# Other SBUF places for the operands of the matmuls of a non-local block

## The reference: what is computed

```
q = theta_w . x + theta_b                    (256 x 1024 positions)
xpool = maxpool2(x)                          (1024 x 256 positions)
k = phi_w . xpool + phi_b                    (256 x 256)
v = g_w . xpool + g_b                        (256 x 256)
p = softmax(q^T k / sqrt(256))               (1024 x 256)
out = z_w . (v p^T) + z_b + x                (1024 x 1024 positions)
```

## The kernel before, in words

| matmuls | stationary | moving | columns |
|---|---|---|---|
| project_q | theta 2 | x_split 3.5 | 512 |
| attend | vt 3.5 | pt 5 | 512 |
| project_out | z 2 | att 5 | 256 |
| project_k | phi 2 | xp 3.5 | 256 |
| project_v | xp 3.5 | g 2 | 256 |
| scores | q 3.5 | k 3.5 | 256 |

## Time and profile before

### The profile page before, as it was taken

The page is one execution under the profiler, slowest core; times in us unless marked ns, Lnnn a source line. Parts: engine busy times, 40 slices in busy tenths (PEclk is TensorE's granted clock), DMA queues, the critical chain, the costliest instruction groups (busy, mean ns, idle before and its releaser), DMA issues.

```text
span 2107.2 us, 41473 instructions
## 1 busy us (share of the span) xinstructions
PE 2084.7 (99%) x14030; PEld 1900.6 (90%) x14030; DVE 1562.8 (74%) x2620; ACT 1294.2 (61%) x2228; POOL 1372.8 (65%) x833
## 2 busy tenths in 40 slices
PE   8899999999999999999999999999999999999997
PEld 7799999999999999999999999999999999999997
DVE  8786776876777867767767778777678677787765
ACT  5566565665666665666656656656666556566553
POOL 4676666776667766666766667666667666676653
PEclk9999999999999999999999999999999999999999
DMA  6556556555566565566564665555665656655535
GB/s 220 176 179 208 170 205 219 189 189 200 169 210 236 166 204 172 196 219 200 180 210 164 210 229 171 203 179 184 219 211 177 209 168 200 229 174 204 184 117 180
DMA packets 212904, 407.22 MB, mean 193 GB/s; under 512 B 12688, under 2 KB 15760, under 8 KB 212880
## 3 DMA queue, kind: packets, MB, share of 16 engines
q1 hardware_dynamic: 212736, 406.90, 57.5%
q10 hardware_dynamic: 144, 0.01, 0.0%
HBM read 272.64 MB, written 134.22 MB: 193 GB/s over the span
## 4 chain that ended last, share of the span: by engine, by line
PE 94%; DVE 3%; POOL 1%; issue 1%; DMA 1%; ACT 1%; DVEq 0%; SPq 0%; ACTq 0%
PE bank L800 94%; DVE pt_raw L633 1%; DMA x<-x 1%; DVE x_top L651 0%; DVE x_bot L651 0%; POOL x_split_lo L520 0%; POOL att_f L533 0%; DVE g_lo L597 0%; POOL att_lo L538 0%; DVE x_split_lo L682 0%; ACT probs L432 0%; PE bank L807 0%; DVE att_f L664 0%; DVE q_lo L611 0%; POOL pt_lo L530 0%
## 5 line engine op out<-in xcount | busy, mean ns | idle before, releaser
L520 POOL TENSOR_TENSOR x_split_lo<-x,x_split_hi 128x1024 fp32r<-128x1024 f32 x254 | 612.6, 2418 | 265.0 <-ACT x_split_hi L335 260.2
L800 PE MATMUL bank<-att_hi,z_hi 128*128 128x256 f32 x1792 | 496.3, 277 | 7.8 <-DVE x_bot L651 4.9
L800 PE MATMUL bank<-att_lo,z_hi 128*128 128x256 f32 x1792 | 495.3, 276 | 0.0
L800 PE MATMUL bank<-att_hi,z_lo 128*128 128x256 f32 x1792 | 495.2, 276 | 0.0
L633 DVE STREAM_TRANSPOSE pt_raw<-probs 32x256 f32<-32x256 f32 x1024 | 446.2, 436 | 18.0 <-ACT probs L432 1.5
L800 PE MATMUL bank<-x_split_hi,theta_hi 128*128 128x512 f32 x1024 | 406.8, 397 | 3.2 <-POOL x_split_lo L520 1.7
L800 PE MATMUL bank<-x_split_lo,theta_hi 128*128 128x512 f32 x1024 | 404.1, 395 | 0.0
L800 PE MATMUL bank<-x_split_hi,theta_lo 128*128 128x512 f32 x1024 | 403.3, 394 | 0.0
L651 DVE TENSOR_TENSOR x_top<-bank,x_top 128x512 f32<-128x512 f32 x512 | 334.5, 687 | 83.1 <-PE bank L800 76.3
L538 POOL TENSOR_TENSOR att_lo<-att_f,att_hi 128x512 fp32r<-128x512 f32 (+1 forms) x192 | 282.9, 1480 | 173.8 <-ACT att_hi L374 173.8
L335 ACT ACTIVATE x_split_hi<-x 128x1024 fp32r<-128x1024 f32 x256 | 270.8, 1058 | 151.6 <-PE bank L800 146.1
(11 more groups left out here) (70 smaller groups left out, 4108.5 us busy)
## 6 DMA issues: line engine op xcount, KB each, us to landing
x<-x SPq DMA_DIRECT2D x256, 512.0 KB, 3.9
x_top<-x SPq DMA_DIRECT2D x128, 512.0 KB, 7.1
x_bot<-x SPq DMA_DIRECT2D x128, 512.0 KB, 5.5
out<-x_top SPq DMA_DIRECT2D x128, 512.0 KB, 3.6
out<-x_bot SPq DMA_DIRECT2D x128, 512.0 KB, 6.7
x_top<-theta_wt SPq DMA_DIRECT2D x4, 256.0 KB, 6.6
x_top<-g_wt SPq DMA_DIRECT2D x4, 256.0 KB, 6.3
x_bot<-z_wt SPq DMA_DIRECT2D x4, 256.0 KB, 6.8
```

The lines of the kernel that those rows point to most:

```text
L520: nc.gpsimd.tensor_tensor(flat(lo), flat(x_chunk(s, c)), raw(flat(hi)), ALU.subtract).then_inc(x_ready, 1)
L800: last = nc.tensor.matmul(dst, stationary(a), moving(b), start=start and n == 0, stop=stop and n == len(PRODUCTS) - 1, skip_group_check=re ...
```

## The change

The order in which the tensors are placed is another one, with a pad of 64 bytes at the start and one of 128 bytes behind g. `still` gets 224 columns in place of 256, and the matmuls of `keep_busy` as many. Nothing else differs: no instruction is added, removed or moved. By the same rules of placing, the places after are:

| matmuls | stationary | moving | columns |
|---|---|---|---|
| project_q | theta 0 | x_split 0 | 512 |
| attend | vt 0 | pt 0 | 512 |
| project_out | z 0 | att 3 | 256 |
| project_k | phi 0 | xp 3 | 256 |
| project_v | xp 3 | g 6 | 256 |
| scores | q 0 | k 3 | 256 |

The tensors that only the other engines use (x, x_top, x_bot, pooled, probs, pt_raw, att_f) come to 0 as well; they were at 3.5, and pt_raw and att_f at 5. The biases, maxima and sums come to between 3 and 6.

```diff
--- before.py
+++ after.py
@@ -65,6 +65,7 @@
 P1, P2, P6, P5, P7, P3, P4 = range(7)
 A_TOP, U_TOP, C11, V_BOT, C22, C12, C21 = range(7)
 SUMS = 14
+STILL = 224
 
 
 def non_local_block(nc, x, theta_wt, phi_wt, g_wt, z_wt, biases, out):
@@ -89,35 +90,37 @@
             return ctx.enter_context(nc.semaphore(name))
 
 
-        theta = [sb(f"theta_{s}", [P, KT, D], f32r) for s in ("hi", "lo")]
-        phi = [sb(f"phi_{s}", [P, KT, D], f32r) for s in ("hi", "lo")]
-        gw = [sb(f"g_{s}", [P, KT, D], f32r) for s in ("hi", "lo")]
-        weights = [theta, phi, gw]
-        zw = [sb(f"z_{s}", [P, 7, TB * P], f32r) for s in ("hi", "lo")]
+        sb("pad_moving", [P, 16], f32)
+        xp = [sb(f"xp_{s}", [P, KT, M], f32r) for s in ("hi", "lo")]
+        k = [sb(f"k_{s}", [P, DT, M], f32r) for s in ("hi", "lo")]
+        att = [sb(f"att_{s}", [P, 7, HB], f32r) for s in ("hi", "lo")]
+
         bias = sb("bias", [P, NB], f32)
         phi_bias = sb("phi_bias", [P, DT], f32)
-
-        xb = [sb(f"x{i}", [P, KC, H], f32) for i in range(XB)]
-
-        xs = [[sb(f"x_split_{s}{i}", [P, KC, H], f32r) for s in ("hi", "lo")] for i in range(XS)]
-
-        x_top = [sb(f"x_top{i}", [P, TB, H], f32) for i in range(2)]
-        x_bot = sb("x_bot", [P, TB, H], f32)
-
-        pooled = sb("pooled", [P, KT, MH], f32)
-        xp = [sb(f"xp_{s}", [P, KT, M], f32r) for s in ("hi", "lo")]
-        q = [sb(f"q_{s}", [P, DT, H], f32r) for s in ("hi", "lo")]
-        k = [sb(f"k_{s}", [P, DT, M], f32r) for s in ("hi", "lo")]
-        vt = [sb(f"vt_{s}", [P, MT, D], f32r) for s in ("hi", "lo")]
-        probs = sb("probs", [P, NT, M], f32)
         negmax = sb("negmax", [P, NT], f32)
         rowsum = sb("rowsum", [P, NT], f32)
         rowinv = sb("rowinv", [P, NT], f32)
+
+        gw = [sb(f"g_{s}", [P, KT, D], f32r) for s in ("hi", "lo")]
+
+        sb("pad_stationary", [P, 32], f32)
+        theta = [sb(f"theta_{s}", [P, KT, D], f32r) for s in ("hi", "lo")]
+        phi = [sb(f"phi_{s}", [P, KT, D], f32r) for s in ("hi", "lo")]
+        zw = [sb(f"z_{s}", [P, 7, TB * P], f32r) for s in ("hi", "lo")]
+        q = [sb(f"q_{s}", [P, DT, H], f32r) for s in ("hi", "lo")]
+        vt = [sb(f"vt_{s}", [P, MT, D], f32r) for s in ("hi", "lo")]
+        pt = [sb(f"pt_{s}", [P, MT, H], f32r) for s in ("hi", "lo")]
+        xs = [[sb(f"x_split_{s}{i}", [P, KC, H], f32r) for s in ("hi", "lo")] for i in range(XS)]
+        weights = [theta, phi, gw]
+
+        xb = [sb(f"x{i}", [P, KC, H], f32) for i in range(XB)]
+        x_top = [sb(f"x_top{i}", [P, TB, H], f32) for i in range(2)]
+        x_bot = sb("x_bot", [P, TB, H], f32)
+        pooled = sb("pooled", [P, KT, MH], f32)
+        probs = sb("probs", [P, NT, M], f32)
         pt_raw = sb("pt_raw", [P, MT, H], f32)
-        pt = [sb(f"pt_{s}", [P, MT, H], f32r) for s in ("hi", "lo")]
         att_f = sb("att_f", [P, 8, HB], f32)
-        att = [sb(f"att_{s}", [P, 7, HB], f32r) for s in ("hi", "lo")]
-        still = sb("still", [P, 256], mybir.dt.bfloat16)
+        still = sb("still", [P, STILL], mybir.dt.bfloat16)
 
 
         bank = [ctx.enter_context(nc.psum_tensor(f"bank{i}", [P, 512], f32)) for i in range(8)]
@@ -804,7 +807,7 @@
             def keep_busy(dst, times):
 
                 for _ in range(times):
-                    nc.tensor.matmul(dst[:, :256], still[:, :P], still[:, :], start=True, stop=True)
+                    nc.tensor.matmul(dst[:, :STILL], still[:, :P], still[:, :], start=True, stop=True)
 
             def project_q(turn, s, c):
```

More of the change, by code:

```diff
@@ L89, in sem @@
             return ctx.enter_context(nc.semaphore(name))
+        sb("pad_moving", [P, 16], f32)
+        xp = [sb(f"xp_{s}", [P, KT, M], f32r) for s in ("hi", "lo")]
+        k = [sb(f"k_{s}", [P, DT, M], f32r) for s in ("hi", "lo")]
+        att = [sb(f"att_{s}", [P, 7, HB], f32r) for s in ("hi", "lo")]
+        bias = sb("bias", [P, NB], f32)
+        phi_bias = sb("phi_bias", [P, DT], f32)
+        negmax = sb("negmax", [P, NT], f32)
+        rowsum = sb("rowsum", [P, NT], f32)
+        rowinv = sb("rowinv", [P, NT], f32)
+        gw = [sb(f"g_{s}", [P, KT, D], f32r) for s in ("hi", "lo")]
+        sb("pad_stationary", [P, 32], f32)
         theta = [sb(f"theta_{s}", [P, KT, D], f32r) for s in ("hi", "lo")]
         phi = [sb(f"phi_{s}", [P, KT, D], f32r) for s in ("hi", "lo")]
-        gw = [sb(f"g_{s}", [P, KT, D], f32r) for s in ("hi", "lo")]
+        zw = [sb(f"z_{s}", [P, 7, TB * P], f32r) for s in ("hi", "lo")]
[3 more added lines that the diff above has]
+        xs = [[sb(f"x_split_{s}{i}", [P, KC, H], f32r) for s in ("hi", "lo")] for i in range(XS)]
         weights = [theta, phi, gw]
-        zw = [sb(f"z_{s}", [P, 7, TB * P], f32r) for s in ("hi", "lo")]
-        bias = sb("bias", [P, NB], f32)
-        phi_bias = sb("phi_bias", [P, DT], f32)
         xb = [sb(f"x{i}", [P, KC, H], f32) for i in range(XB)]
-        xs = [[sb(f"x_split_{s}{i}", [P, KC, H], f32r) for s in ("hi", "lo")] for i in range(XS)]
         x_top = [sb(f"x_top{i}", [P, TB, H], f32) for i in range(2)]
@@ L107, in non_local_block @@
         pooled = sb("pooled", [P, KT, MH], f32)
-        xp = [sb(f"xp_{s}", [P, KT, M], f32r) for s in ("hi", "lo")]
-        q = [sb(f"q_{s}", [P, DT, H], f32r) for s in ("hi", "lo")]
-        k = [sb(f"k_{s}", [P, DT, M], f32r) for s in ("hi", "lo")]
-        vt = [sb(f"vt_{s}", [P, MT, D], f32r) for s in ("hi", "lo")]
         probs = sb("probs", [P, NT, M], f32)
-        negmax = sb("negmax", [P, NT], f32)
-        rowsum = sb("rowsum", [P, NT], f32)
-        rowinv = sb("rowinv", [P, NT], f32)
         pt_raw = sb("pt_raw", [P, MT, H], f32)
-        pt = [sb(f"pt_{s}", [P, MT, H], f32r) for s in ("hi", "lo")]
         att_f = sb("att_f", [P, 8, HB], f32)
-        att = [sb(f"att_{s}", [P, 7, HB], f32r) for s in ("hi", "lo")]
-        still = sb("still", [P, 256], mybir.dt.bfloat16)
+        still = sb("still", [P, STILL], mybir.dt.bfloat16)
         bank = [ctx.enter_context(nc.psum_tensor(f"bank{i}", [P, 512], f32)) for i in range(8)]
```

## The result

The change makes the kernel faster: 2095.27 us (median of 4 runs, 2093.23 to 2095.40) against 2109.15 (4 runs), a ratio of 0.9931 with a 95% interval of 0.9919 to 0.9942. I had said 2060, and 2032 to 2088: the sign is right, the size is less than a third, and the time lies outside the range.

The account below looks back on a forecast made before the run. TensorE was taken to bound the kernel, time being matmul count times pitch. 26.4 us (256 columns) plus 27.3 (512 columns) less 3.7 gave 50.0 us off 2108.98: 2059, stated as 2060, range 2032 to 2088.

Parts of the forecast that it names:

- 512 columns at distance 0 on a line, 226.6 ns: project_q and attend: pitch from 233.7 to 226.6 ns over 3840 matmuls, a gain of 27.3 us.
- the first rival: 512-column classes: a matmul's extra is paid once, not per column; pitch 219.9 ns, 2034 us; chance 0.16.
- the second: Rival: the 512-column classes gain nothing, their extra being neither line nor load; 2085 us; chance 0.18.
- the fourth: Rival, 512-column classes: load and columns collide at distance 0; pitch 247.9 ns, slower at 2137 us; chance 0.08.
- project_out. The distance stays 3, both stay on a line: 0.: project_out, 5376 matmuls of 256 columns: pitch stays at 113.3 ns, so no gain or loss.
- scores and project_k at project_out's 113.3: 256-column classes brought to distance 3: scores gains 10.3 us and project_k 10.0.
- project_v at 113.3: 256-column class brought to distance 3: pitch from 117.3 to 113.3 ns, a gain of 6.1 us.
- what the off-line operand then costs: Reason for 226.6: an operand half a line off costs 7.1 ns at 512 columns, beside 6.7, 6.5 and 4.0 elsewhere.
- The seam at distance 0: From project_v to project_q, g's columns beside theta's load, both at 2: 0.11 us, read as project_out's pitch.
- Place has no say: Rival for all classes: the places of operands don't affect the pitch; 2109 us, no change; chance 0.08.
- Covers: Other engines' work stays hidden: 0.77 us left ahead of scores, 1.0 ahead of attend, so no wait comes up.
- 3.7 us given away at start and end: First 100 and last 47.2 us, where TensorE waits for others: all of the gain there counted as lost.

Follow-up runs that it names:

- part_512: Kernel before the change, with only the operands of the 512-column classes moved to distance 0: 2109.65 us, ratio 1.0003.
- off_512: Changed kernel, with the columns of the two 512-column classes (x_split and pt) put 1.5 lines on, back to distance 1.5: 2091.54 us, ratio 0.9916.
- The maps: TensorE alone, no attention block: 12 matmuls per pair of weight and column places, 0 to 7.5 lines in half lines; 512 columns 226.7 ns at distance 0.
- entry_map: TensorE alone, no attention block: 6 matmuls of 512 columns at a, then 18 of 256 at b, weights at 0; b = 3 gave 113.3 or 117.8 ns.

## Why the prediction was wrong

- *TensorE bounds, and time is count times pitch*: right. Between 100 and 2040 us TensorE never waits, and the differences in pitch add up to -15.2 us where the span fell by 13.7.
- *512 columns at distance 0 on a line, 226.6 ns*: right, 226.7, but the number was chosen over 219.9 for what an off-line operand costs, and that reason is wrong (below). The extra above the bare columns is 13.4 ns here and 6.6 at 256, so the first rival is out; at 226.7 the second and the fourth are as well. The fixed 2.5 ns that the Trainium skill (TensorE: Matmul & The Clock Gate, section Back-to-back issue gap) gives for a matmul in isolation fits neither.
- *"project_out. The distance stays 3, both stay on a line: 0."* This step failed, and it is most of the error. It measured 117.8 in place of 113.7, +22.0 us. I had weighed that the place might count rather than the distance. What I had not seen is a third thing: the pair in force doesn't fix the pitch, the run ahead has a say. The 512-column runs that gained 26 us enter project_out so that it takes the slow pattern. part_512 shows it with project_out's places untouched (117.8), off_512 the way back (113.7).
- *scores and project_k at project_out's 113.3*: the same failure. They are at 117.8, 1536 x 4.5 ns each, 13.8 us together, and at 113.6 and 113.3 in off_512 at the same places.
- *project_v at 113.3*: right within 0.5 ns, but by luck: it is entered from the slow scores, and in off_512, entered from the quick one, it had 117.9.
- *"what the off-line operand then costs"*, the reason that I gave: wrong. The maps show a period of 4 lines in the distance and no cost of the half line as such. The seam at distance 0 was one matmul long, and in entry_map a 256-column run that stays at distance 0 settles at 120.0; so the row couldn't carry what I rested on it.
- *Place has no say*, the third rival: out. The Trainium skill (SBUF — State Buffer, section Who interferes with whom) says that PE waits for no one and that its two read ports are independent. The map, with TensorE alone, has 226.7 to 235.0 ns by the distance of the two operands, so the pitch does depend on where the two lie. Whether it is the two reads that meet, no run here shows.
- *Covers*: right, 0.77 us left ahead of scores, nothing came up.
- *3.7 us given away at start and end*: near in size, but the drop of the clock at 88.3 us, some 2 us, was not in it.

The trace of before held a warning. The first matmul of project_out's runs takes 117 ns, the second 116, only then 113 to 114. A pitch that needs four matmuls to settle is a state that is entered, and a change ahead of it can keep it from being entered. A row of single starts would have hinted at that; I divided runs by their count.

The 22.0 and 13.8 us come to 35.8, and 35.3 lie between 2060 and 2095.3; the other differences nearly cancel. What the two patterns are inside TensorE or the memory is open. That it is the load of the next weights meeting the columns of the running matmul fits the dependence on their distance, but no run here separates the two.

## What to carry to other kernels

Where TensorE is full and each matmul has its own weight load, the places of the two operands are worth a per cent or two: take the pitch of each class from starts in the timeline, and compare classes of the same shape. Don't price a placement by its own pair alone: the same pair ran at 113.3 or 117.8 ns by what ran ahead, so a placement is tried as a whole sequence, first with TensorE alone and in the kernel's order, which here gave one kernel time within 2 us ahead of its run and accounts for another within 1. And look at the first few distances of a run: if they drift, the steady pitch may depend on the entry.

## What the runs showed of the hardware

- float32r matmuls with a weight load each, at full clock: 226.7 ns for 512 columns at best, 228.8 to 235.0 at other distances of columns and weights; 256 columns 113.3 at best, 116.2 to 120.4 elsewhere.
- The distance counts modulo 256 bytes; a common shift of all operands by 128 bytes changed nothing (2095.13 against 2095.27 us).
- At a distance of 3 lines of 64 bytes, 256 columns have two stable patterns, 113.3 and 117.8 ns. One weight load in 36 at another place can switch between them: with the same slice at line 3 the kernel lost 10 us, at line 5.5 it gained 22.
